# Checking four guessed recurrence streams on TensorE and ScalarE, and sharing the final adds out anew

## The chip, the cores and the metric

The kernel runs on one core of a Trainium2 chip. The metric is device time in microseconds (us). The engines are PE (TensorE, matrix products), PEld (its weight loads), DVE (VectorE), ACT (ScalarE), POOL (GpSimd) and SP (SyncE, which here only issues DMAs).

## The reference, cut to what matters

The input x is (16, 32, 32, 32) in fp32. First an attention-like block over a layer norm of x is added to x; then comes a feed-forward block that holds a recurrence over 1024 tokens:

```
x = x + conv_ref(ln(x), ...)            # scores, softmax, weighted values
t = x.reshape(16, 1024, 32)
Wx = batchnorm(ln(t) @ W.T) * gamma + beta
y = 0
for each token: y = sigmoid(Wx_t + y @ V.T); ys.append(y)
out = t + ys
```

The loop is sequential: each of its 1024 states needs the one before.

## The kernel before, in words

Everything stays in the on-chip memory of 128 partitions. Images and features lie on the partitions (G = 4 groups of C = 32), and the four groups of images Q = 4, the rows i and the columns lie along the free axis. The attention block, the second layer norm (`x2` is what the recurrence's result is added to) and the batch norm fill the time up to about 106 us.

**The recurrence.** It is not run token after token. The 1024 tokens are cut in 128 segments of SEG = 8, and all segments run at once, as STREAMS = 4 streams that each hold 32 segments of 4 groups of images (128 columns). A segment doesn't know the state it starts from, so ROUNDS = 17 rounds are run: WARM = 9 rounds, which run the tokens ahead of a segment from a guess and leave the start states in `warm`, and then 8 rounds whose states are kept in `states`. In each round and for each stream PE multiplies the last state by V (L1186) into a PSUM bank that was seeded with Wx (L933 on DVE), and ACT takes the sigmoid (L680). The four streams follow one another in the order that `order(WARM)` gives.

**The end.** A stream keeps 8 rows, and they are finished in PIECES: rows 0 to 3, rows 4 and 5, rows 6 and 7. For each piece `finish` (L945) waits for the states, transposes them 32x32 on DVE into `back` (`turn_back`, L356), and then adds `x2` (`add_back`, L362, one line for both engines). The list ON_DVE says which adds DVE does: one of the four of the first piece, and two of four of the others. POOL does the other seven. So DVE's program at the end is: 4 transposes of 128x512, one add of 512 columns, 4 transposes of 128x256, two adds of 256, 4 transposes of 256, two adds of 256, and then the check.

**The check.** The start states that were guessed are right if the last kept state of each segment agrees with the warm-up's last. DVE takes the difference of the 128x512 states (L965), squares and sums it along each partition (L969), and compares each partition's sum with AGREE squared, 2 to the power of -36 (L972). PE counts the partitions that agree (L1190), DVE turns the count into a flag (L974), and every engine but POOL loads the flag into a register (L345 on SP, L977 on DVE, L686 on ACT, L1192 on PE) and branches. When any partition disagrees, a loop of 127 passes over all streams computes the recurrence again; else the branch is skipped.

**The stores.** SP issues eight stores of 256 KB (L341): first rows 0 to 3 of each stream, then rows 4 to 7 of each, each after its adds (`wait_added`). It loads the flag only after it has issued all of them, and ends when they have landed. POOL's last work is its adds; before them it sets constants early on (`average`, L405) and works in the attention block and the layer norms.

Of the kernel before, what the change touches and what calls it, by code (L numbers as in the profile page):

```python
# [5 lines left out]
P = 128  # L6
G = 4
Q = 4
C = 32
# [16 lines left out]
ON_DVE = [(0, 3), (1, 1), (1, 3), (2, 1), (2, 3)]  # L26
PIECES = [(0, 4), (4, 2), (6, 2)]
STORES = [(0, 0, 4), (2, 4, 4)]
AGREE = 2.0 ** -18
LN1_EPS = 1e-6  # L30
LN2_EPS = 1e-5
# [10 lines left out]
def metaformer_kernel(nc, x, Wq, Wk, Wv, rq, rk, rv, Gq, Gk, Gv1, Gv2, W, V, gamma, beta, out):  # L42
# [4 lines left out]
    with ExitStack() as ctx:  # L47
        def sb(name, shape, dt=F32):
            return ctx.enter_context(nc.sbuf_tensor(name, shape, dt))
# [59 lines left out]
        nought = sb("nought", [P, C])  # L109
        ones = sb("ones", [P, 1])  # L110
        blank = sb("blank", [P, BANK], BF16)
        bn = sb("bn", [P, UNITS, 6])
        bnv = sb("bnv", [P, 8])
        std, scl, shift = (bnv[:, k:k + 1] for k in range(5, 8))
# [6 lines left out]
        diff = square[:, :, :].rearrange("p b (k m) -> p (b k) m", k=2)  # L121
# [6 lines left out]
        names = """x_in0 x_in1 x_in2 x_in3 x_in4 wqk_in w_in r_in_s rv_in gates_in gates2_in affine_in zeros average_set  # L128
# [10 lines left out]
        diff_d diff_sum agreed agree_count flag  # L139
        f_marked f_start f_seeded f_preact f_state f_turned""".split()  # L140
        S = {n: sem(n) for n in names}
        block = ctx.enter_context(nc.Block())
# [87 lines left out]

            return STREAMS * t + order(t).index(r) + 1

        STORED = 16 * len(STORES) * STREAMS
        FINAL_SIDE = side(WARM - 1)
        WARM_BANK = 0

# [28 lines left out]
            else:  # L265
                eng.wait_ge(S["seeded"], DVE_SEEDED.index((n, r)) + 1)

        def added_on_dve(n, r):

            return (n, order(WARM).index(r)) in ON_DVE  # L270

        ADDS = [(n, r) for n in range(len(PIECES)) for r in order(WARM)]

        def wait_added(eng, n, r):

            for own in (True, False):
                before = [k for k, a in enumerate([a for a in ADDS if added_on_dve(*a) == own]) if a[1] == r and a[0] <= n]
                if before:
                    eng.wait_ge(S["added_dve"] if own else S["added_pool"], before[-1] + 1)

        @block.sync
        def _(sp):
# [51 lines left out]
            for n in range(CHUNKS):  # L334
                spread_att(n)

            for n, row, k in STORES:
                for r in order(WARM):
                    wait_added(sp, n, r)
                    rows = slice(SEG * r + row, SEG * r + row + k)  # L340
# [9 lines left out]
            sp.wait_ge(S["stored"], STORED)  # L350

        def turn_back(row, k, r):

            rows = slice(SEG * r + row, SEG * r + row + k)
            at = P * (SEG * r + row)
            return nc.vector.transpose(back[:, at:at + P * k].rearrange("p (q i j) -> p i q j", q=Q, i=k),  # L356
                                       states[:, rows, :, :])

        def add_back(eng, row, k, r):
            rows = slice(SEG * r + row, SEG * r + row + k)  # L360
            at = P * (SEG * r + row)
            return eng.tensor_tensor(result[:, :, rows, :], back[:, at:at + P * k].rearrange("p (q i j) -> p q i j", q=Q, i=k),  # L362
                                     x2[:, :, rows, :], ALU.add)

        @block.gpsimd
        def _(pool):
# [37 lines left out]
            for k in range(1 - G, G):  # L404
                nc.gpsimd.affine_select(out=average[:, :, :], in_=average[:, :, :], compare_op=ALU.not_equal,  # L405
                                        fill=1.0 / G, base=C * k, pattern=[[-C, G], [-1, C]],
                                        channel_multiplier=1).then_inc(S["average_set"], 1)
                pool.wait_ge(S["average_set"], k + G)

            def shift_scores(n):  # L410
                pool.wait_ge(S["score_max"], n + 1)
# [52 lines left out]
            scale(6)  # L464
            scale(7)

            for n, r in ADDS:
                if not added_on_dve(n, r):
                    pool.wait_ge(S["turned_back"], ADDS.index((n, r)) + 1)
                    add_back(nc.gpsimd, *PIECES[n], r).then_inc(S["added_pool"], 1)  # L470

        @block.scalar
        def _(act):
# [198 lines left out]
            for t in range(ROUNDS):  # L672
                for r in order(t):
                    if t == 0:

                        nc.scalar.activation(state_out(t, r), wx_q[:, SEG * r + round_row(t), :, :],  # L676
                                             ACT.Sigmoid, bias=first_shift, scale=scl).then_inc(S["state"], 1)
                    else:
                        act.wait_ge(S["preact"], count(t, r) - STREAMS)
                        nc.scalar.activation(state_out(t, r), rec_slot(t, r).rearrange("p (q c) -> p q c", q=Q),  # L680
                                             ACT.Sigmoid).then_inc(S["state"], 1)
                if t == 0:
                    act_seeds(0)

            act.wait_ge(S["flag"], 1)
            repeat = act.value_load(repeat_flag[0:1, 0:1], min_val=0, max_val=1)  # L686
# [10 lines left out]
        def _(dve):  # L697
# [245 lines left out]
                    seed(n, r).then_inc(S["seeded"], 1)  # L943

            def finish(n):  # L945

                row, k = PIECES[n]
# [3 lines left out]
                for r in order(WARM):  # L951
                    if added_on_dve(n, r):
                        dve.wait_ge(S["turned_back"], ADDS.index((n, r)) + 1)
                        add_back(nc.vector, row, k, r).then_inc(S["added_dve"], 1)


            for n in range(len(SEEDS)):
                seeds(n)
            for n in range(len(PIECES)):
# [14 lines left out]
            nc.vector.tensor_scalar(repeat_flag[:, :], ps[0:1, 0, 0:1], float(P), None,  # L974
                                    ALU.is_lt).then_inc(S["flag"], 1)
            dve.wait_ge(S["flag"], 1)
            repeat = dve.value_load(repeat_flag[0:1, 0:1], min_val=0, max_val=1)  # L977
            with dve.If(repeat == 1):
                PASS = SEG * STREAMS
                dve.wait_ge(S["f_marked"], 1)  # L980
                with dve.Fori(0, SEGMENTS - 1) as n:

                    nc.vector.tensor_copy(warm[:, FINAL_SIDE, :, :, 1:C + 1], states[:, SEG - 1::SEG, :, :]).then_inc(S["f_start"], 1)
                    for h in range(GROUPS):
                        for r in range(STREAMS):
                            seed(len(SEEDS) - GROUPS + h, r).then_inc(S["f_seeded"], 1)
                    dve.wait_ge(S["f_state"], n * PASS + PASS)
                dve.wait_ge(S["stored"], STORED)
                for h in range(GROUPS):
                    for r in range(STREAMS):  # L990
                        n = GROUPS * (STREAMS * h + r)
                        turn_back(ROWS * h, ROWS, r).then_inc(S["f_turned"], 1)
                        dve.wait_ge(S["f_turned"], n + 1)
                        add_back(nc.vector, ROWS * h, ROWS, r).then_inc(S["f_turned"], 1)
                        dve.wait_ge(S["f_turned"], n + 2)

        @block.tensor
        def _(pe):
# [181 lines left out]
            for t in range(1, ROUNDS):  # L1180
                for r in order(t):
                    if t == 1 or SEED_OF[t] > SEED_OF[t - 1]:
# [52 lines left out]
```

## Time and profile before

| | us |
|---|---|
| runs of the kernel | 134.37, 137.07, 137.10 (median 137.07) |
| the profiled execution | 134.09 |
| its span, first to last instruction | 132.3 |
| granted TensorE clock, mean share of full | 0.98 |
| POOL, DVE, PE, ACT busy | 67.9, 95.3, 101.9, 79.4 |

The span is what the trace covers; the 1.8 us between it and the 134.09 us lie around it. A time "at 122.84" is counted from the start of the span. Where neighbouring instructions on DVE or POOL overlap by some hundredths, the later one's start is in the pipeline of the one before.

### The profile page before, as it was taken

What the parts mean: (1) busy time and instruction counts of PE and PEld (TensorE: products, weight loads), DVE (VectorE), ACT (ScalarE), POOL (GpSimd) and SP (SyncE); (2) the same over time, 40 slices, a digit from 0 to 9 for tenths busy, and PEclk for the clock granted to TensorE, in tenths of its full rate; (3) what the DMA queues carried; (4) which work ended last, traced back from release to release, by engine and by line L of the source; (5) the groups of instructions that cost most, each with busy time, mean ns of one, the idle gap of its engine ahead of it and who ended that gap; (6) DMA issues with size and microseconds to landing.
All of it is one profiled execution on the core that took longest, in us unless ns stands there. A gap on an engine that the chain in (4) does not pass through costs nothing.

```text
span 132.3 us, 4756 instructions
## 1 busy us (share of the span) xinstructions
PE 101.9 (77%) x2078; PEld 74.9 (57%) x2080; DVE 95.3 (72%) x151; ACT 79.4 (60%) x162; POOL 67.9 (51%) x77
## 2 busy tenths in 40 slices
PE   0694997799779999887995996756959969999000
PEld 0331232169779999775994995421312449999000
DVE  5898928857210396897790595799999597889991
ACT  7967874970913546598892512442652699999100
POOL 8996863994000057528700998998960000008840
PEclk9999999999999999999999999999999999999975
DMA  3892651084000000060061000000000000002666
GB/s 147 249 319 23 152 126 40 0 202 128 0 5 5 5 7 5 9 143 19 5 136 27 5 5 5 5 0 0 0 0 0 0 0 0 5 2 58 198 178 201
DMA packets 7968, 7.98 MB, mean 60 GB/s; under 512 B 2124, under 2 KB 6220, under 8 KB 7948
## 3 DMA queue, kind: packets, MB, share of 16 engines
q1 hardware_dynamic: 7948, 7.69, 22.0%
q8 instruction: 16, 0.26, 0.9%
q14 instruction: 4, 0.03, 0.1%
HBM read 2.97 MB, written 2.10 MB: 38 GB/s over the span
## 4 chain that ended last, share of the span: by engine, by line
PE 25%; POOL 22%; DVE 22%; ACT 13%; issue 7%; DMA 6%; SPq 2%; POOLq 0%; ACTq 0%; DVEq 0%
POOL y_tile L437 6%; ACT warm L680 5%; PE ps L1036 5%; PE ps L1072 4%; POOL u_tile L431 4%; DVE xin L356 4%; POOL y_tile L443 4%; PE ps L1051 4%; PE ps L1084 3%; DVE y_tile L362 3%; PE ps L1028 3%; POOL y_tile L196 3%; DMA spread_parts<-rel_tile 3%; PE ps L1060 3%; DMA xin<-in_x_dram 3%
## 5 line engine op out<-in xcount | busy, mean ns | idle before, releaser
L412 POOL TENSOR_TENSOR att_tile<-att_tile,soft 128x1024 f32<-128x1024 f32 x4 | 7.8, 1955 | 20.6 <-DVE soft L784 20.6
L362 POOL TENSOR_TENSOR y_tile<-xin,u_tile 128x256 f32<-128x256 f32 (+1 forms) x7 | 7.1, 1045 | 20.8 <-DVE xin L356 20.8
L1036 PE MATMUL ps<-spread_parts,u_tile 128*32 128x64 f32 x512 | 12.9, 252 | 2.0 <-issue 2.0
L1036 PEld LDWEIGHTS ps<-spread_parts,u_tile 128*32 128x32 f32 x512 | 12.2, 190 | 2.4 <-issue 2.4
L933 DVE TENSOR_SCALAR ps<-att_tile,bnv 128x512 f32<-128x512 f32 x15 | 11.0, 807 | 1.6 <-ACT warm L680 1.6
L1072 PE MATMUL ps<-spread_parts,rv_t 128*32 128x128 f32 x256 | 11.2, 339 | 0.9 <-DMA spread_parts<-rel_tile 0.9
L1084 PE MATMUL ps<-spread_parts,v_tile 128*32 128x64 f32 x512 | 9.0, 222 | 3.3 <-issue 3.2
L1095 PE MATMUL ps<-rel_tile,w_bd 128*128 128x512 f32 x16 | 8.7, 623 | 3.2 <-DVE rel_tile L848 2.5
L1072 PEld LDWEIGHTS ps<-spread_parts,rv_t 128*32 128x32 f32 x256 | 10.3, 119 | 1.4 <-issue 1.1
L1148 PE MATMUL ps<-blank 128*128 128x512 bf16 x40 | 9.8, 379 | 1.5 <-DVE u_tile L826 1.3
L778 DVE TENSOR_TENSOR att_tile<-ps,rel_tile 128x1024 f32<-128x1024 f32 x4 | 4.9, 1214 | 8.4 <-ACT rel_tile L513 8.4
L611 ACT ACTIVATE square<-y_tile 128x512 f32<-128x512 f32 x8 | 5.0, 628 | 9.6 <-POOL y_tile L437 9.6
L1084 PEld LDWEIGHTS ps<-spread_parts,v_tile 128*32 128x32 f32 x512 | 8.4, 109 | 3.9 <-issue 3.8
L1028 PE MATMUL ps<-y_tile,m_fac 32*32 32x512 f32 x64 | 7.7, 592 | 3.8 <-DVE y_tile L196 2.0
L1051 PE MATMUL ps<-spread_parts,r_fac 128*32 128x128 f32 x256 | 10.0, 315 | 0.0
L1008 PE MATMUL ps<-xin 128*128 128x512 f32 x18 | 9.9, 690 | 0.0
L1186 PE MATMUL ps<-warm,w_bd 128*128 128x128 f32 x72 | 9.0, 281 | 1.0 <-ACT warm L676 0.6
L513 ACT COPY rel_tile<-ps 128x512 f32<-128x512 f32 x8 | 4.8, 602 | 8.2 <-PE ps L1051 8.2
L1051 PEld LDWEIGHTS ps<-spread_parts,r_fac 128*32 128x32 f32 x256 | 9.6, 115 | 0.0
L583 ACT COPY spread_parts<-rel_tile 32x1024 f32<-32x1024 f32 x8 | 8.5, 1064 | 1.8 <-POOL rel_tile L419 1.5
L1186 PEld LDWEIGHTS ps<-warm,w_bd 128*128 128x128 f32 x72 | 8.4, 191 | 1.9 <-DVE ps L933 1.5
L431 POOL TENSOR_TENSOR u_tile<-att_tile,u_tile 128x512 f32<-128x512 f32 x4 | 5.2, 1330 | 7.4 <-ACT att_tile L604 7.4
(112 smaller groups left out, 242.2 us busy)
## 6 DMA issues: line engine op xcount, KB each, us to landing
out_dram<-y_tile SPq DMA_DIRECT2D x8, 256.0 KB, 2.3
xin<-in_x_dram SPq DMA_DIRECT2D x3, 512.0 KB, 4.6
spread_parts<-att_tile SPq DMA_DIRECT2D x8, 128.0 KB, 2.4
spread_parts<-rel_tile SPq DMA_DIRECT2D x8, 128.0 KB, 2.8
xin<-in_x_dram SPq DMA_DIRECT2D x2, 256.0 KB, 2.8
spread_parts<-u_tile SPq DMA_DIRECT2D x4, 128.0 KB, 2.3
att_tile<-in_L_conv_rv_dram SPq DMA_DIRECT2D x4, 128.0 KB, 3.0
att_tile<-in_L_conv_rq_dram SPq DMA_DIRECT2D x1, 128.0 KB, 6.1
```

The costliest lines, as they stand in the source:

```text
L362: return eng.tensor_tensor(result[:, :, rows, :], back[:, at:at + P * k].rearrange("p (q i j) -> p q i j", q=Q, i=k), x2[:, :, rows, :], A ...
L431: nc.gpsimd.tensor_tensor(unit(x2, k), first_sums[:, k, :, :], unit(x2, k), ALU.add).then_inc(S["x2_added"], 1)
L933: return nc.vector.tensor_scalar(out, rows, scl, shift, ALU.mult, ALU.add)
L1008: ins = nc.tensor.matmul(bank(k), xin[:, 0, 0:4, :].rearrange("p i j -> p (i j)"), xin[:, 0, 0:16, :].rearrange("p i j -> p (i j)"), start ...
L1028: ins = nc.tensor.matmul(bank(SIDE[k])[p, :], m_fac[p, :], y_tile[p, IMG * q + BANK * k:IMG * q + BANK * (k + 1)], start=True, stop=True)
L1036: return nc.tensor.matmul(ps[group(q), first + j // 8, at:at + G * HALF].rearrange("p (g i) -> p g i", g=G), u[:, q, :, j], y_bd[:, q, :, ...
L1051: ins = nc.tensor.matmul(side_bank(n)[group(q), P * k:P * (k + 1)].rearrange("p (g jp t) -> p g jp t", g=G, t=RUN), r_fac[:, ROWS * n + k, ...
L1072: ins = nc.tensor.matmul(bank(4 + n % 4)[group(g), P * k:P * (k + 1)].rearrange("p (q jp t) -> p q jp t", q=Q, t=RUN), rv_t[:, ROWS * n + ...
L1084: ins = nc.tensor.matmul(ps[group(g), first + j // 8, at:at + Q * HALF].rearrange("p (q i) -> p q i", q=Q), v_t[:, j, g, :], att_bd[:, g, ...
L1095: nc.tensor.matmul(bank(WX_BANK[k % 2]), w_bd[:, 1, :], by_row(tokens, k), start=True, stop=True).then_inc(S["wx_product"], 1)
L1148: ins = nc.tensor.matmul(bank(k), blank[:, 0:P], blank[:, :], start=True, stop=True)
L1186: nc.tensor.matmul(rec_slot(t, r), w_bd[:, 2, :], state_in(t, r), start=False, stop=True, skip_group_check=True).then_inc(S["preact"], 1)
```

## The change

The check leaves DVE. POOL makes a 128x128 unit matrix and its negative early on (`signs`). When all states are there, PE multiplies the last states by the first and the warm-up's last states by the second, both into PSUM bank 1, which then holds the difference; ACT squares that bank with a sum along each partition. DVE keeps the two small comparisons, and they now stand between its adds. PIECES, ON_DVE and STORES go: the transposes keep the three pieces (TURNED), with rows 4 to 7 written into one block of `back`; POOL adds rows 0 to 3 of all four streams, and DVE adds rows 4 to 7 of all four, in one instruction of 512 columns each, after all its transposes. The stores are the same eight.

```diff
+TURNED = [(0, 4), (4, 2), (6, 2)]
...
         def wait_added(eng, n, r):
+            eng.wait_ge(S["added_dve" if n else "added_pool"], order(WARM).index(r) + 1)
...  (SP)
-            for n, row, k in STORES:
+            for n in range(GROUPS):
                 for r in order(WARM):
                     wait_added(sp, n, r)
...
         def turn_back(row, k, r):
+            at = COLS // C * (SEG * r + row - row % ROWS)
+            block4 = back[:, at:at + BANK].rearrange("p (q i j) -> p i q j", q=Q, i=ROWS)
+            return nc.vector.transpose(block4[:, row % ROWS:row % ROWS + k], states[:, SEG * r + row:SEG * r + row + k, :, :])
...  (POOL, early)
+            nc.gpsimd.memset(signs[:, :, :], 0.0).then_inc(S["signs_zero"], 1)
+            pool.wait_ge(S["signs_zero"], 1)
+            for n, unit_value in enumerate((1.0, -1.0)):
+                nc.gpsimd.affine_select(out=signs[:, n, :], in_=signs[:, n, :], compare_op=ALU.not_equal, fill=unit_value, base=0,
+                                        pattern=[[-1, P]], channel_multiplier=1).then_inc(S["signs_set"], 1)
...  (POOL, end)
+            for i, r in enumerate(order(WARM)):
+                pool.wait_ge(S["turned_back"], i + 1)
+                add_back(nc.gpsimd, 0, r).then_inc(S["added_pool"], 1)
...  (ACT, after the recurrence)
+            act.wait_ge(S["diff_product"], 1)
+            nc.scalar.activation(square[:, 0, 0:BANK], bank(1), ACT.Square, accum_out=diffsum[:, :]).then_inc(S["diff_sum"], 1)
...  (DVE)
-            dve.wait_ge(S["state"], STREAMS * ROUNDS)
-            nc.vector.tensor_tensor(diff[:, 0, :].rearrange("p (r q c) -> p r q c", r=STREAMS, q=Q),
-                                    states[:, SEG - 1::SEG, :, :], warm[:, FINAL_SIDE, :, :, 1:C + 1],
-                                    ALU.subtract).then_inc(S["diff_d"], 1)
-            dve.wait_ge(S["diff_d"], 1)
-            nc.vector.tensor_tensor_reduce(diff[:, 1, :], diff[:, 0, :], diff[:, 0, :], 1.0, 0.0,
-                                           ALU.mult, ALU.add, diffsum[:, :]).then_inc(S["diff_sum"], 1)
+            def finish_adds(streams):
+                for i, r in streams:
+                    dve.wait_ge(S["turned_back"], STREAMS * (len(TURNED) - 1) + i + 1)
+                    add_back(nc.vector, 1, r).then_inc(S["added_dve"], 1)
...
+            streams = list(enumerate(order(WARM)))
+            finish_adds(streams[0:2])
             dve.wait_ge(S["diff_sum"], 1)
             nc.vector.tensor_scalar(agreed[:, :], diffsum[:, :], AGREE * AGREE, None, ALU.is_le).then_inc(S["agreed"], 1)
+            finish_adds(streams[2:3])
             dve.wait_ge(S["agree_count"], 1)
             nc.vector.tensor_scalar(repeat_flag[:, :], ps[0:1, 0, 0:1], float(P), None,
                                     ALU.is_lt).then_inc(S["flag"], 1)
+            finish_adds(streams[3:4])
...  (PE)
+            pe.wait_ge(S["signs_set"], 2)
+            pe.wait_ge(S["state"], STREAMS * ROUNDS)
+            nc.tensor.matmul(bank(1).rearrange("p (r m) -> p r m", r=STREAMS), signs[:, 0, :],
+                             states[:, SEG - 1::SEG, :, :].rearrange("p r q c -> p r (q c)"), start=True, stop=False)
+            nc.tensor.matmul(bank(1).rearrange("p (r q c) -> p r q c", r=STREAMS, q=Q), signs[:, 1, :],
+                             warm[:, FINAL_SIDE, :, :, 1:C + 1], start=False, stop=True).then_inc(S["diff_product"], 1)
```

## Rows read from the trace of the kernel before

**Rows 1.** The page's chain that ended last, shares of the span by engine.
```profile
PE 25%; POOL 22%; DVE 22%; ACT 13%; issue 7%; DMA 6%; SPq 2%; POOLq 0%; ACTq 0%; DVEq 0%
```

**Rows 2.** Timeline of ACT from 115.7 us: start us, us, engine, line, operation, count.
```profile
115.61 7.23 ACT L680 ACTIVATE v_tile<-ps 128x128 f32<-128x128 f32 x32
```

**Rows 3.** The chain of waits after 115 us: start us, us it adds, what.
```profile
118.60 2.50 DVE xin L356 x4
121.12 1.31 DVE y_tile L362
122.44 1.33 DVE xin L356 x4
123.77 1.62 DVE y_tile L362 x2
125.39 1.33 DVE xin L356 x4
126.72 1.12 DVE y_tile L362 x2
127.84 0.61 DVE square L965
128.48 0.69 DVE square L969
129.65 0.14 DVE repeat_flag L974
```

**Rows 4.** Lines 977 and 47, sequencer instructions: count, ns min/median/max, first and last start.
```profile
L977 DVEq TENSOR_LOAD <-repeat_flag x1: 1177/1177/1177, 129.8 to 129.8; - x1
L47 SPq DRAIN  x1: 13/13/13, 131.8 to 131.8; - x1
L47 DVEq DRAIN  x1: 51/51/51, 132.0 to 132.0; - x1
```

**Rows 5.** Line 341, the sixth and the last store, each with its time to landing.
```profile
L341 SPq DMA_DIRECT2D out_dram<-y_tile x1: 373/373/373, 127.5 to 127.5; - x1
DMA to landing us min/median/max: 2.3/2.3/2.3
...
L341 SPq DMA_DIRECT2D out_dram<-y_tile x1: 543/543/543, 128.5 to 128.5; - x1
DMA to landing us min/median/max: 3.1/3.1/3.1
```

**Rows 6.** Busy time by window: PE, PEld, DVE, ACT, POOL, PEclk, DMA share, GB/s.
```profile
123.00:127.00 4.00, 0.00 (x0) 0.00 (x0) 4.00 (x10) 0.00 (x0) 3.28 (x5) 1.00 0.64 188
127.00:132.00 5.00, 0.19 (x2) 0.09 (x2) 2.44 (x7) 0.00 (x0) 0.23 (x1) 0.51 0.73 210
```

**Rows 7.** Timeline of the adds between 119 and 123 us, read in narrow windows.
```profile
119.39 1.27 POOL L362 TENSOR_TENSOR y_tile<-xin,u_tile 128x512 f32<-128x512 f32 x1 [20.05 <-DVE xin L356]
120.62 1.26 POOL L362 TENSOR_TENSOR y_tile<-xin,u_tile 128x512 f32<-128x512 f32 x1
121.12 1.31 DVE L362 TENSOR_TENSOR y_tile<-xin,u_tile 128x512 f32<-128x512 f32 x1
121.85 1.71 POOL L362 TENSOR_TENSOR y_tile<-xin,u_tile 128x512 f32<-128x512 f32 x1
```

**Rows 8.** Timeline: one fp32 product of 512 columns (L1095) on PE, and ACT's nearest operations.
```profile
96.36 1.10 PE L1095 MATMUL ps<-rel_tile,w_bd 128*128 128x512 f32 x2 [0.59 <-ACT att_tile L624]
...
91.17 0.63 ACT L611 ACTIVATE square<-y_tile 128x512 f32<-128x512 f32 x1 [0.78 <-POOL y_tile L437]
...
104.80 1.28 ACT L658 ACT_TABLE_LOAD   x1
106.09 0.20 ACT L658 ACTIVATE table_load<-bn_eps 128x1 f32<-128x1 f32 x1
```

**Rows 9.** Timeline of POOL from 27 us: the constants, and the idle time behind them.
```profile
28.97 3.05 POOL L405 TENSOR_SCALAR_AFFINE_SELECT average<-average 128x128 f32<-128x128 f32 x7
47.78 1.95 POOL L412 TENSOR_TENSOR att_tile<-att_tile,soft 128x1024 f32<-128x1024 f32 x1 [15.77 <-DVE soft L784]
```

More of the change, by code:

```diff
@@ L25 @@
 LN_PARTS = [(0, 0, 16), (0, 16, 16), (1, 0, 32), (2, 0, 32), (3, 0, 32)]
-ON_DVE = [(0, 3), (1, 1), (1, 3), (2, 1), (2, 3)]
-PIECES = [(0, 4), (4, 2), (6, 2)]
-STORES = [(0, 0, 4), (2, 4, 4)]
+TURNED = [(0, 4), (4, 2), (6, 2)]
 AGREE = 2.0 ** -18
@@ L111, in metaformer_kernel @@
         blank = sb("blank", [P, BANK], BF16)
+        signs = sb("signs", [P, 2, P])
         bn = sb("bn", [P, UNITS, 6])
@@ L120, in metaformer_kernel @@
         table_load = sb("table_load", [P, 1])
-        diff = square[:, :, :].rearrange("p b (k m) -> p (b k) m", k=2)
         agreed = sb("agreed", [P, 1])
@@ L126, in metaformer_kernel @@
         ps = ctx.enter_context(nc.psum_tensor("ps", [P, 8, BANK], F32))
-        names = """x_in0 x_in1 x_in2 x_in3 x_in4 wqk_in w_in r_in_s rv_in gates_in gates2_in affine_in zeros average_set
+        names = """x_in0 x_in1 x_in2 x_in3 x_in4 wqk_in w_in r_in_s rv_in gates_in gates2_in affine_in zeros average_set signs_zero signs_set
         spread_zero0 spread_zero1 spread_zero2 spread_zero3 y_in0 y_in1 y_in2 y_copied_dve y_copied_act att_in0 att_in1 att_copied
@@ L138, in metaformer_kernel @@
         warm_zero warmed seeded preact state turned_back added_dve added_pool stored
-        diff_d diff_sum agreed agree_count flag
+        diff_product diff_sum agreed agree_count flag
         f_marked f_start f_seeded f_preact f_state f_turned""".split()
@@ L231, in count @@
             return STREAMS * t + order(t).index(r) + 1
-        STORED = 16 * len(STORES) * STREAMS
+        STORED = 16 * GROUPS * STREAMS
         FINAL_SIDE = side(WARM - 1)
@@ L266, in wait_seeded @@
                 eng.wait_ge(S["seeded"], DVE_SEEDED.index((n, r)) + 1)
-        def added_on_dve(n, r):
-            return (n, order(WARM).index(r)) in ON_DVE
-        ADDS = [(n, r) for n in range(len(PIECES)) for r in order(WARM)]
         def wait_added(eng, n, r):
[L276 to L279, printed above, removed]
+            eng.wait_ge(S["added_dve" if n else "added_pool"], order(WARM).index(r) + 1)
         @block.sync
@@ L335, in _ @@
                 spread_att(n)
-            for n, row, k in STORES:
+            for n in range(GROUPS):
                 for r in order(WARM):
                     wait_added(sp, n, r)
-                    rows = slice(SEG * r + row, SEG * r + row + k)
+                    rows = slice(SEG * r + ROWS * n, SEG * r + ROWS * (n + 1))
                     sp.dma_start(out_dram[:, :, C * rows.start:C * rows.stop],
@@ L352, in turn_back, with add_back @@
         def turn_back(row, k, r):
[L354 to L362, printed above, removed]
+            at = COLS // C * (SEG * r + row - row % ROWS)
+            block4 = back[:, at:at + BANK].rearrange("p (q i j) -> p i q j", q=Q, i=ROWS)
+            return nc.vector.transpose(block4[:, row % ROWS:row % ROWS + k], states[:, SEG * r + row:SEG * r + row + k, :, :])
+        def add_back(eng, n, r):
+            rows = slice(SEG * r + ROWS * n, SEG * r + ROWS * (n + 1))
+            at = COLS // C * rows.start
+            return eng.tensor_tensor(result[:, :, rows, :], back[:, at:at + BANK].rearrange("p (q i j) -> p q i j", q=Q, i=ROWS),
                                      x2[:, :, rows, :], ALU.add)
@@ L465, in _ @@
             scale(7)
[L467 to L470, printed above, removed]
+            for i, r in enumerate(order(WARM)):
+                pool.wait_ge(S["turned_back"], i + 1)
+                add_back(nc.gpsimd, 0, r).then_inc(S["added_pool"], 1)
         @block.scalar
@@ L945, in finish @@
             def finish(n):
-                row, k = PIECES[n]
+                row, k = TURNED[n]
                 for r in order(WARM):
@@ L950, in finish @@
                     turn_back(row, k, r).then_inc(S["turned_back"], 1)
[L951 to L954, printed above, removed]
+            def finish_adds(streams):
+                for i, r in streams:
+                    dve.wait_ge(S["turned_back"], STREAMS * (len(TURNED) - 1) + i + 1)
+                    add_back(nc.vector, 1, r).then_inc(S["added_dve"], 1)
             for n in range(len(SEEDS)):
                 seeds(n)
-            for n in range(len(PIECES)):
+            for n in range(len(TURNED)):
                 finish(n)
-            dve.wait_ge(S["state"], STREAMS * ROUNDS)
-            nc.vector.tensor_tensor(diff[:, 0, :].rearrange("p (r q c) -> p r q c", r=STREAMS, q=Q),
-                                    states[:, SEG - 1::SEG, :, :], warm[:, FINAL_SIDE, :, :, 1:C + 1],
-                                    ALU.subtract).then_inc(S["diff_d"], 1)
-            dve.wait_ge(S["diff_d"], 1)
-            nc.vector.tensor_tensor_reduce(diff[:, 1, :], diff[:, 0, :], diff[:, 0, :], 1.0, 0.0,
-                                           ALU.mult, ALU.add, diffsum[:, :]).then_inc(S["diff_sum"], 1)
+            streams = list(enumerate(order(WARM)))
+            finish_adds(streams[0:2])
             dve.wait_ge(S["diff_sum"], 1)
             nc.vector.tensor_scalar(agreed[:, :], diffsum[:, :], AGREE * AGREE, None, ALU.is_le).then_inc(S["agreed"], 1)
+            finish_adds(streams[2:3])
             dve.wait_ge(S["agree_count"], 1)
@@ L993, in _ @@
                         dve.wait_ge(S["f_turned"], n + 1)
-                        add_back(nc.vector, ROWS * h, ROWS, r).then_inc(S["f_turned"], 1)
+                        add_back(nc.vector, h, r).then_inc(S["f_turned"], 1)
                         dve.wait_ge(S["f_turned"], n + 2)
```

## The prediction

> **What bounds the kernel now.** I read the page's chain first: no engine holds more than a quarter of it [rows 1], so a change at one place is worth what the last wait at that place is worth, and nothing more. The change leaves everything before the last states alone, apart from three constants on POOL. So I read ACT's timeline for the moment from which the tail runs: 32 sigmoids in 7.23 us, one each 0.22 us, the last of them ending at 122.84 [rows 2]. That moment stays. From there the chain of waits is DVE alone: transposes and adds until 127.84, the difference and its square for about 1.3 us, then the two small comparisons, with the flag at 129.79 [rows 3]. That would say: take work off DVE and gain all of it.
>
> Two more views say that it isn't so. The sequencer rows show that loading the flag takes 1.18 us and that DVE drains at 132.0, just before the end at 132.25; SP drains at 131.85 [rows 4]. So two paths end together: flag to end is 132.25 - 129.83 = 2.42 us on DVE, and the stores are the other. The last store is issued at 128.54 and lands 3.1 us later, at 131.64; the sixth, issued at 127.54, needs only 2.3 and lands at 129.84 [rows 5]. The eighth is two places behind the sixth: (131.64 - 129.84) / 2 = 0.90 us a store. That is a queue: a store issued while another is under way lands 0.90 us after it, not 2.3 us after its issue. The window after 127 us has the DMA engines busy for 73% of the time, a stretch of it without any store [rows 6]. So a faster flag is worth nothing unless the stores come earlier too, and how early they come is set by when each add ends.
>
> **The change, part by part.**
>
> *Constants on POOL.* A memset and two selects over 128x128; seven such selects took 3.05 us, 0.44 each [rows 9], so some 1.3 us. POOL idles for 15.77 us behind them [rows 9]. They cost nothing; without that cover they would cost their 1.3 us.
>
> *DVE's transposes.* The first four end at 121.10, as now [rows 3]. The add that follows goes, so the eight small ones come next: two groups of four at 1.33 us [rows 3] end at 121.10 + 2.66 = 123.76. The last round's states are there at 122.16 to 122.84 (0.22 apart, back from the last, rows 2), and the last group starts at 122.43, so it never waits for one. Their writes into blocks of four rows change only a step; I cost that at nothing.
>
> *POOL's adds.* Four of 512 columns, at 1.23 us from start to start [rows 7], from 119.39: the fourth ends at 119.39 + 4 x 1.23 + 0.04 = 124.35. Now the first store group is complete at 124.0, since DVE does one of the four; this is the part that becomes slower.
>
> *DVE's first two adds.* A DVE add beside a POOL add is not free: at 121.12 it took 1.31 us, ending at 122.43, where the POOL add before it ended at 121.88; the difference is 0.55, the time of an add by itself (0.61 for L965, rows 3). And the POOL add that began at 121.85 took 1.71 in place of 1.27 [rows 7]. I read this as turns, not as sharing: whoever starts second stands still. So the first DVE add, issued at 123.7, waits for POOL and ends at 124.35 + 0.55 = 124.90; the second, undisturbed, at 125.51. If both were slowed instead, POOL's fourth would end 0.44 later, at 124.8. The Trainium skill ("SBUF — State Buffer", section "Who interferes with whom") says that a VectorE instruction with two SBUF inputs and a GpSimd instruction that reads SBUF exclude one another for the whole instruction, first come first served; by it POOL's fourth add isn't lengthened, and the trace agrees, with 1.26 us for the POOL add that the DVE add ran into.
>
> *The check on PE and ACT.* No product of this kind is in the trace. One fp32 product of 512 columns took 1.10 us [rows 8], two 2.20; the lower bound is that the second is hidden in the pipeline by half, about 1.6, the upper that PE has fallen to 1.2 GHz, 4.4. PE stands idle for 4 us after the recurrence at a granted clock of 1.00 and only in the next window is it 0.51 [rows 6], and here it gets work at once: I take 2.20, and PE ends at 122.84 + 0.05 + 2.20 = 125.09. ACT's square of 512 columns took 0.63 [rows 8]; reading out the sum is not shown, between 0.08 (DVE's whole step behind L969 takes no more) and a small ACT instruction of 0.20 [rows 8]; I take 0.20, the like engine. The sum is there at 125.96. What waits behind it on DVE is two adds and, through them, the last two stores.
>
> *DVE's end.* It stands 0.4 us for the sum, compares (0.15) until 126.15, adds until 126.76, sets the flag (0.14, rows 3) at 126.90, with PE's count long done in between, and adds until 127.51. The flag load follows at 127.54 at the latest and ends the program on DVE at 127.54 + 2.42 = 129.96.
>
> *The stores.* With 2.3 us for one that meets none and 0.90 behind another: the fourth is issued at 124.38 and lands at 126.7. The fifth (124.93) would land at 127.2 and is queued to 127.6, the sixth (125.54) to 128.5, the seventh (126.79) to 129.4, the eighth (127.54) to 130.3, where by itself it would have landed at 129.85. SP issues the same eight instructions, each some 0.4 us, so none is delayed by the queue's own time. A delay of the check up to 0.45 us is thus hidden.
>
> *The sum.* The last landing was 131.64 with the end at 132.25; SP's drain comes 0.2 after the landing, and the final barrier takes 0.2 to 0.25. The new end is 130.3 + 0.45 = 130.75, and DVE's path, 129.96, is covered by 0.8. That is 1.5 us less than the 132.25, or 132.6 for the profiled execution of 134.09. The runs lie at 134.4 once and at 137.1 twice, so the median stands 3.0 above the profiled execution for reasons that no row shows; the forecast for a median is **137.07 - 1.5 = 135.6 us**, 1.1% less.
>
> **The rivals.**
>
> *A. The gain is smaller, because the fourth POOL add or the check comes late.* Slowed by DVE, POOL's fourth ends at 124.8; every later store moves by 0.44 and the end is 131.2, a gain of 1.05. For it: 1.71 us in [rows 7]. Or a function table is loaded for the square: the table is the sigmoid's, and one load took 1.28 us [rows 8]. If it stands behind ACT's wait, the sum comes at 127.24, the last add ends at 128.79, and the last store lands at 128.8 + 2.3 = 131.1, or 131.2 in the queue: a gain of 0.6. Against it: the squares of the norms ran without a load of their own beside the square root. Time: 136.0 to 136.5.
>
> *B. The gain is larger.* If the queue's 0.90 shrinks when stores come more evenly spaced, the last lands at 129.85 and the end is 130.3, or DVE's own 129.96 if SP's end is quicker: a gain of 2.0 to 2.3, 134.8 to 135.1. Against it: stores five to seven still come within 2.3 us of each other.
>
> *C. Tables change twice around the square,* to its set and back to the sigmoid's, both between ACT's wait and the sum: 2 x 1.28 = 2.57 us [rows 8]. The sum comes at 128.53, the eighth store is issued at 130.11 and lands at 132.4, and the end is 132.85: **slower by 0.6 us**, 137.7. It decides when the sum comes 2.0 us or more after my 125.96, since 132.25 - 0.45 - 2.3 = 129.5 is the latest issue that costs nothing, 1.96 after mine. For the price of a change of table the trace has 1.28 us, the activation behind it starting 0.01 later [rows 8]. The Trainium skill ("ScalarE: Activation LUTs", section "What ACT_TABLE_LOAD costs") adds a drain and calls a change about 2.66 us; by this one change alone would make the kernel slower by some 0.7 us. The trace doesn't show that drain.
>
> *D. The products don't reproduce the difference exactly,* so that a partition exceeds 2 to the power of -36 and the repeat loop runs. The limit over 512 elements is a root mean square of 2^-18 / 22.6 = 1.7e-7, near the last bits of an fp32 number below 1, so rounding in the products could reach it. The price: 127 passes of 8 rounds of 4 sigmoids at 0.22 us [rows 2] are at least 894 us, over 1,030 in all. Against it: a product with one and minus one has nothing to round if PE carries all bits, and the two PE instructions for each fp32 product [rows 8] speak for that.
>
> **How the numbers follow.** The forecast has 0.58, A 0.20, B 0.12, C 0.06, D 0.04. The likeliest, 135.6, stands. For the range: the runs before lie at two levels, 134.1 to 134.4 and 137.1, and the new kernel may fall on either. On the lower B gives 134.2 - 2.2 = 132.0; on the upper A's small end gives 136.5 and no gain 137.1. I take 132.0 to 137.2; C and D are left out. A measurement of this kernel can tell about 2% from no change, 2.7 us here. No case gives that much gain by its own; the two levels of the runs could, if the medians fall apart: faster 0.17. Slower by over 2% are D and the wrong fall of the levels: 0.07. Within 2%: 0.76.
>
> **What would show it.** In the profile after: the last sigmoid at about 122.8; eight transposes back to back until 123.8; four POOL adds, none over 1.3 us, until 124.35; the first DVE add ending near 124.9; PE's products until 125.1 and no ACT_TABLE_LOAD before the square; a wait on DVE of some 0.4 us before line L972's successor; the flag at 126.9 against 129.8; the last store issued at 127.5 and landing 2.8 us later; the end by SP and not by DVE. The prediction is wrong if the recurrence itself ends at another time, if the queue lands stores other than 0.9 apart, or if DVE stands for over 0.9 us at the sum.

## The result, and the profile after

The changed kernel runs in 133.69 us (median of 20 runs) against 135.16 for the kernel before on 20 runs. The fast runs of both, compared alone, give a ratio of 0.988, with a 95% interval of 0.984 to 0.992. It is faster by about 1.5 us; the interval allows 1.1 to 2.1. Forecast were 1.5 us and a ratio of 0.989. The level forecast, 135.6 us, rested on the first three runs of the kernel before and was 1.9 us too high; each kernel's runs scatter over some 4 us. The changed kernel's profiled execution took 134.51 us, with a span of 132.7.

The spans can't be compared as they stand: in the changed kernel's trace the last sigmoid ends 1.6 us later than in the one before, at 124.44 in place of 122.84 [rows 2], though nothing on its path was changed. In the 14 traces of this study that moment lies anywhere from 121.7 to 125.0. So I count everything from there. The time from the last sigmoid's end to the end of the span, the **tail**, is 9.42 us before and 8.25 after, 1.17 less.

The chain of waits at the end of the changed kernel (start us, us it adds, what):

```profile
124.00 0.46 ACT v_tile L673 x2
...
124.59 1.10 PE ps L1181 x2
125.69 0.87 PE ps L1183 x2
126.58 0.70 ACT square L679 x2
127.30 0.15 DVE agreed L959
127.45 0.60 DVE y_tile L350
128.11 0.60 DVE y_tile L350
```

DVE's difference and square of [rows 3] are gone, and two adds stand behind the sum that PE and ACT now make. The timeline of the same stretch, each engine's part of it:

```profile
121.00 4.96 POOL L350 TENSOR_TENSOR y_tile<-xin,u_tile 128x512 f32<-128x512 f32 x4 [20.06 <-DVE xin L345]
...
125.23 1.28 DVE L350 TENSOR_TENSOR y_tile<-xin,u_tile 128x512 f32<-128x512 f32 x1
...
127.07 0.19 ACT L679 ACTIVATION_READ_ACCUMULATOR square<-ps 128x1 f32 x1
127.30 0.15 DVE L959 TENSOR_SCALAR agreed<-diffsum 128x1 f32<-128x1 f32 x1 [0.19 <-ACT square L679]
127.97 0.14 DVE L962 TENSOR_SCALAR repeat_flag<-ps 1x1 int32<-1x1 f32 x1
```

POOL's four adds keep their 1.24 us each; where [rows 7] had one of 1.71, none is lengthened. DVE's first add starts while POOL's fourth is under way and takes 1.28. No ACT_TABLE_LOAD stands before the square, and DVE waits 0.19 us for the sum. The last two stores (line 331) with their times to landing, and the sequencers' ends:

```profile
L331 SPq DMA_DIRECT2D out_dram<-y_tile x1: 372/372/372, 128.1 to 128.1; - x1
DMA to landing us min/median/max: 3.0/3.0/3.0
...
L331 SPq DMA_DIRECT2D out_dram<-y_tile x1: 462/462/462, 128.7 to 128.7; - x1
DMA to landing us min/median/max: 3.6/3.6/3.6
...
L966 DVEq TENSOR_LOAD <-repeat_flag x1: 1154/1154/1154, 128.1 to 128.1; - x1
L45 DVEq DRAIN  x1: 45/45/45, 130.3 to 130.3; - x1
L45 SPq DRAIN  x1: 13/13/13, 132.5 to 132.5; - x1
```

The drains stand at the end of each engine's program. In [rows 4] DVE drained last, at 132.0, with SP at 131.85. Now DVE is done 2.2 us ahead of SP: the flag's path is far off the end, and the stores alone set it. The last one takes 3.6 us to land, although it is issued 0.65 us behind the seventh.

The steps in numbers, in us after the end of the last sigmoid (a store has landed when its semaphore is raised):

| | forecast | changed | before |
|---|---|---|---|
| transposes done | 0.92 | 0.87 | 3.9 |
| POOL's last add of rows 0 to 3 | 1.51 | 1.52 | 0.7 |
| DVE's first, second add of rows 4 to 7 | 2.06, 2.67 | 2.07, 2.67 | |
| PE's products, sum ready | 2.25, 3.12 | 2.10, 2.82 | |
| flag | 4.06 | 3.66 | 6.96 |
| last store issued | 4.70 | 4.29 | 5.70 |
| stores 4 to 8 landed | 3.86, 4.76, 5.66, 6.56, 7.46 | 3.91, 4.80, 5.73, 6.63, 7.86 | 3.96, 6.09, 7.05, 7.97, 8.85 |
| end of the span | 7.91 | 8.25 | 9.42 |

### The profile page after: what moved, and what is told of

It reads as the page before. It is cut to its first block, busy times and chain, and to the rows that moved or that the text cites. A ratio compares the mean times of both kernels' runs of the same rounds, so it can differ in the third digit from the quotient of the medians.

```text
span 132.7 us, 4763 instructions
## 1 busy us (share of the span) xinstructions
PE 104.9 (79%) x2082; PEld 76.5 (58%) x2084; DVE 92.8 (70%) x147; ACT 79.7 (60%) x164; POOL 66.6 (50%) x77
## 4 chain that ended last, share of the span: by engine, by line
PE 30%; POOL 22%; ACT 17%; DVE 11%; issue 7%; DMA 5%; SPq 4%; POOLq 0%; ACTq 0%
PE ps L1040 7%; POOL y_tile L431 6%; ACT v_tile L673 5%; ACT warm L673 5%; PE ps L1025 5%; PE ps L1061 4%; POOL u_tile L425 4%; POOL y_tile L437 4%; PE ps L1073 3%; DMA xin<-in_x_dram 3%; PE ps L1017 3%; POOL y_tile L195 3%; PE ps L1049 3%; SPq L297 2%; DMA spread_parts<-rel_tile 2%
## 5 line engine op out<-in xcount | busy, mean ns | idle before, releaser
L350 POOL TENSOR_TENSOR y_tile<-xin,u_tile 128x512 f32<-128x512 f32 x4 | 5.0, 1271 | 20.1 <-DVE xin L345 20.1
L997 PE MATMUL ps<-xin 128*128 128x512 f32 x18 | 10.7, 745 | 0.0
```

The source lines that it names most:

```text
L997: ins = nc.tensor.matmul(bank(k), xin[:, 0, 0:4, :].rearrange("p i j -> p (i j)"), xin[:, 0, 0:16, :].rearrange("p i j -> p (i j)"), start ...
```

## The experiments

All tails below are read in one profile per kernel. They are steadier than the times: two profiles of the changed kernel gave 8.25 and 8.28, two of the candidate (run 7) 7.32 both times, but two of the kernel with the later flag (run 5) 7.91 and 8.12, while the times of one kernel scatter by 4 us. A difference of 0.2 us between two tails is thus not safe where the last store is what differs. Where a timed ratio disagrees with a tail, I say so.

**1. The check alone.** The adds, the transposes and the stores of before, the check of after:

```diff
-            dve.wait_ge(S["state"], STREAMS * ROUNDS)
-            nc.vector.tensor_tensor(diff[:, 0, :]...).then_inc(S["diff_d"], 1)
-            dve.wait_ge(S["diff_d"], 1)
-            nc.vector.tensor_tensor_reduce(diff[:, 1, :], ...).then_inc(S["diff_sum"], 1)
+   (PE's two products, ACT's square, POOL's signs as in the change)
```

> Only the check moves to PE and ACT; the adds and stores stay as before. I count from the end of the last sigmoid to the end of the span: 9.42 us before, 8.25 us in the changed kernel. Theory Q (the end is set by the store queue: a store lands 2.3 us after its issue, or 0.9 us after the store before it): the stores are issued as before, the last lands 8.85 us after the last sigmoid, and the tail is 9.2 us, a gain of 0.2 us. Theory D (DVE's time until the flag sets the end, the flag plus 2.42 us): DVE loses 1.4 us and the tail is 8.0 us.

The tail was 9.64 us, the ratio 1.005 (0.999 to 1.012). Theory D, 8.0 us, is out: taking 1.4 us off DVE gained nothing. Theory Q's stores came as expected, except for the last, which landed at 9.24 in place of 8.85, so the tail grew by 0.2 us in place of shrinking by as much:

```profile
L341 SPq DMA_DIRECT2D out_dram<-y_tile x1: 547/547/547, 128.2 to 128.2; - x1
DMA to landing us min/median/max: 3.5/3.5/3.5
```

**2. The adds alone.** From the changed kernel; DVE's check goes behind its four adds:

```diff
-            finish_adds(streams[0:2])
+            finish_adds(streams)
+            (line 964 to 970 of the kernel before: the difference and its square on DVE)
             dve.wait_ge(S["diff_sum"], 1)
-            finish_adds(streams[2:3])
-            finish_adds(streams[3:4])
```

> Only the adds and stores move; the check stays on DVE, behind all adds. Theory Q: the adds end 2.1, 2.7, 3.3 and 3.9 us after the last sigmoid, the last store lands at 7.5 as in the forecast, and the flag, at 5.95, ends the kernel at 8.4 by its own 2.42 us: a tail of 8.4 us, 1.0 less than before, so most of the change's gain is the adds'. Theory D says the same 8.4 here only if the flag is late; it would give the adds no part in the changed kernel's gain of 1.2 us beyond DVE's shorter list of instructions.

The tail was 8.10 us, the ratio 0.988 (0.973 to 1.003). The last store landed at 7.48. The adds by themselves give 1.32 us, more than the whole change. The flag at 5.82 ended it, as expected; its path took 2.28 us and not 2.42.

**3. The changed kernel again.** No edit.

> The changed kernel once more. In its first profile the last store landed 1.23 us after the seventh, where the others stood 0.90 apart. If that was chance, it lands 0.9 us after it here and the tail is 7.9 us; if it belongs to this order of stores, the tail is 8.2 us again.

The last store landed 1.25 us behind the seventh and the tail was 8.28 us: no chance. The ratio was 0.995 (0.989 to 1.001), whose interval meets the first comparison's.

**4. No check.** The two products and the square are left out:

```diff
+            nc.gpsimd.memset(diffsum[:, :], 0.0).then_inc(S["diff_sum"], 1)     (POOL, early)
-            (PE's two products, ACT's square)
```

> The two products and the square are left out and the sum is set to zero early, so DVE never waits for it; the two comparisons, the count and the flag stay. Theory Q: the last two adds end 0.2 to 0.4 us earlier, the store queue hides it, and the tail stays that of the changed kernel, 7.9 to 8.2 us. The rival (DVE's wait for the sum is paid in full): 0.2 to 0.4 us less.

Both were wrong. The tail grew to 9.65 us, with less work in it, and the timed ratio agrees: 1.000 (0.994 to 1.006), no gain left over the kernel before. The last store was issued 4.01 us after the last sigmoid, earlier than in the changed kernel, and took 5.2 us; it landed 2.6 us behind the seventh. What else moved? The flag, to 3.39, the earliest of all. The page names two DMA queues of kind "instruction". Here is what each holds from 129.0 us on (packets, MB, share of 16 engines), after the store's bulk has passed at 129.1:

```profile
q1 hardware_dynamic: 128, 0.06, 8.1%
q8 instruction: 1, 0.02, 2.2%
q14 instruction: 1, 0.01, 0.7%
```

and the windows of that end (PE, PEld, DVE, ACT, POOL, PEclk, DMA share, GB/s):

```profile
128.00:129.00 1.00, 0.00 (x0) 0.00 (x0) 0.00 (x0) 0.00 (x0) 0.00 (x0) 0.50 1.02 286
129.00:130.00 1.00, 0.00 (x0) 0.00 (x0) 0.00 (x0) 0.00 (x0) 0.00 (x0) 0.50 0.27 78
130.00:130.90 0.90, 0.00 (x0) 0.00 (x0) 0.00 (x0) 0.00 (x0) 0.00 (x0) 0.50 0.04 5
```

The queue runs full until 129, then nearly empties, and a last few packets of 512 bytes pass after 130. Between lies the 16 KB instruction packet, from 129.40 to 130.37 in its record. From 130.38 us on eight packets start, all of them the last store's:

```profile
DMA packets 8, 0.00 MB, mean 6 GB/s; under 512 B 1, under 2 KB 8, under 8 KB 8
```

Theory F came from here: the branch behind the flag makes an engine fetch instructions, and a part of the last store stands behind the fetch on one of the DMA engines. In this run the packets bear that out. In the changed kernel they don't as it stands: its last data packet ends at 7.40 and its 16 KB packet starts at 7.41, and from 131.86 us on no packet starts:

```profile
DMA packets 0, 0.00 MB, mean 0 GB/s; under 512 B 0, under 2 KB 0, under 8 KB 0
```

So no packet of that store waited behind the large one, and yet it landed 0.35 us later than in run 6 below, which has no fetch. Its last five data packets end 0.047 us apart, the last of them at 7.40 in place of 7.16, and the landing follows 0.46 us behind it in place of 0.35. Why is open.

**5. The flag later.** All adds ahead of the comparisons:

```diff
-            finish_adds(streams[0:2])
+            finish_adds(streams)
             (agreed)
-            finish_adds(streams[2:3])
             (flag)
-            finish_adds(streams[3:4])
```

> The changed kernel with all four of DVE's adds ahead of the two comparisons, so the flag comes at 4.5 us after the last sigmoid in place of 3.66. Theory F: after the branch the engines fetch instructions by DMA (16 KB, 0.96 us of one DMA engine); where that is asked for while the last store is still under way, some 2.5 us after the flag and before 7.1, a part of the last store stands behind it and it lands 1.23 us after the seventh and not 0.9. Here the fetch is asked for at about 7.0: the last store lands at 7.5 and the tail is 7.9 us, 0.35 less than the changed kernel, though the flag is later. Rival (the flag's time costs or is hidden, no fetch): the tail stays 8.25 us or grows.

The flag came at 4.37 in place of 3.66, the last store landed at 7.52, 0.88 us behind the seventh, and the tail was 7.91 us: 0.34 less for a later flag. The last store of this kernel:

```profile
L331 SPq DMA_DIRECT2D out_dram<-y_tile x1: 853/853/853, 127.5 to 127.5; - x1
DMA to landing us min/median/max: 3.6/3.6/3.6
```

It was issued 0.4 us earlier than the changed kernel's and would have landed no earlier for that in the queue; what it gained is the 0.34. A repetition (12 below) kept only 0.13 of it.

**6. No branch.** The flag is computed, but nobody loads it, and the repeat loops are left out:

```diff
-            X.wait_ge(S["flag"], 1)
-            repeat = X.value_load(repeat_flag[0:1, 0:1], min_val=0, max_val=1)
-            with X.If(repeat == 1): ...      (X: SP, ACT, DVE, PE)
```

> The changed kernel without the four loads of the flag and without the repeat loops behind them (the flag is still computed). Theory F: no jump, no late fetch, the last store lands 0.9 us after the seventh at 7.5 and the tail is 7.9 us or a little under. Rival (the last store is slow in this order of stores whatever follows): it lands at 7.86 and the tail is 8.2 us.

With all issues where the changed kernel has them (the last at 4.29), the last store landed at 7.51 and the tail was 7.92 us. The answer on DMAs for its tail, from 124.0 us to the end, names one queue alone:

```profile
DMA packets 4120, 2.04 MB, mean 230 GB/s; under 512 B 128, under 2 KB 4120, under 8 KB 4120
## 3 DMA queue, kind: packets, MB, share of 16 engines
q1 hardware_dynamic: 4120, 2.04, 79.8%
```

No instruction packet, no delay. The edit takes out the loads of the flag, the branches and the code of the loops together, so it doesn't say by itself which of them it is. The loads alone are unlikely: in run 2 DVE's lies at 5.86 to 6.86, while the data of the last two stores move, and the last was not late. The timed ratio, 0.999 (0.995 to 1.004), doesn't show the 1.5 us that the tail lost. The trace has its last sigmoid at 124.97, the latest of all; whether the shorter program makes the part before slower is open.

**7. POOL adds three.** A candidate, 11 a repetition of it:

```diff
+TURNS = 4 of (0, i), 4 of (1, i), then (2, 0) to (2, 3)
+DVE_ADDS = [(0, 2), (1, 0), (1, 1), (1, 2), (1, 3)]
+POOL_ADDS = [(0, 0), (0, 1), (0, 3)]
...  (DVE)
+            turn(0, 0) ... turn(0, 3); turn(1, 0); turn(1, 1)
+            add(0, 2)
+            turn(1, 2); turn(1, 3); turn(2, 0); turn(2, 1)
+            add(1, 0); add(1, 1)
+            turn(2, 2); turn(2, 3)
+            add(1, 2); add(1, 3)
+            (agreed, flag)
```

> A candidate. DVE adds rows 0 to 3 of the third stream between its transposes, POOL the other three; the transposes of the last two rows alternate with DVE's adds; the check comes after all adds. Theory Q with F: the third and fourth stores are issued at -0.4 and 0.75 us against 0.32 and 1.55 now, the fifth at 1.5, the last at 3.95; the queue lands the last at 6.65, the flag is there at 4.55 and ends DVE at 6.85: a tail of 7.0 to 7.1 us, 1.2 us less than the changed kernel and 2.3 less than before (1.7%). Rival (POOL and DVE slow each other, so that moving an add to DVE delays its transposes and every store): a tail of 8.2 us or more.

The tail was 7.32 us and the ratio 0.987 (0.979 to 0.995). The issues came as expected (-0.35, 0.77, 1.55, ... 4.01), the landings didn't: from the second store on, at 1.46, they stand 0.87 to 0.95 apart to the last, at 6.93. I had let the queue begin with the fourth store. It begins with the second now, and the tail is the time to move 1.5 MB.

**8. Half of each store** (groups of images 0 and 1 alone):

```diff
-                    sp.dma_start(out_dram[:, :, C * rows.start:C * rows.stop], result[:, :, rows, :]...)
+                    sp.dma_start(out_dram[:, 0:2, C * rows.start:C * rows.stop], result[:, 0:2, rows, :]...)
```

> The changed kernel with half of each store left out (two of the four groups of images, 128 KB each). Theory Q: a store occupies the DMA engines for 0.45 us and not 0.9, no store stands behind another, and the last lands 2.0 to 2.3 us after its issue at 4.29, at 6.3 to 6.6. Rival (the spacing of 0.9 us is the cost of one store instruction whatever its size): the last lands at 7.5 to 7.9 again.

```profile
L331 SPq DMA_DIRECT2D out_dram<-y_tile x1: 372/372/372, 127.9 to 127.9; - x1
DMA to landing us min/median/max: 1.8/1.8/1.8
```

The last landed 1.81 us after its issue, at 6.10, and the tail was 6.49 us: it landed 0.2 us sooner than expected, since a store that meets none is itself 0.5 us shorter. The 0.9 us is the time that 256 KB take, about 290 GB/s, not the cost of an instruction.

**9. The check late:**

```diff
+            for _ in range(3):
+                nc.tensor.matmul(bank(1)..., signs[:, 0, :], states..., start=True, stop=False)
+                nc.tensor.matmul(bank(1)..., signs[:, 1, :], warm..., start=False, stop=True)
```

> The changed kernel with PE's pair of products made four times over before ACT squares the bank, 0.86 us a pair, so the sum comes 2.6 us later, at about 5.4 us after the last sigmoid in place of 2.83. Theory Q: the seventh and the last store are issued at 6.2 and 6.9 us, the last lands 2.3 us after its issue, at 9.2, and the tail is 9.6 us, 1.3 more than the changed kernel (1.7 more than with a last store at 7.5): half or more of a late check is paid, since two adds stand behind it. Rival (the check is hidden behind the store queue however late): 8.25 us.

I had mis-sized the edit: 0.86 us is one product back to back, not a pair (the chain above adds 0.87 for the second), so the sum came 5.15 us later, at 7.97. By Q's own rule with the stores issued at 8.78 and 9.44, the last lands at 12.0 and the tail is 12.4. The tail was 14.28: the last store took 4.45 us:

```profile
L331 SPq DMA_DIRECT2D out_dram<-y_tile x1: 372/372/372, 131.2 to 131.2; - x1
DMA to landing us min/median/max: 4.4/4.4/4.4
```

The instruction packet ran from 11.90 to 12.86, and three packets of the last store end behind it, at 12.92 to 13.04. That is theory F's delay once more, 1.9 us of it, in a queue that had stood empty before. The windows around it (same columns):

```profile
132.50:133.60 1.10, 0.00 (x0) 0.00 (x0) 0.00 (x0) 0.00 (x0) 0.00 (x0) 0.50 0.72 206
133.60:134.60 1.00, 0.00 (x0) 0.00 (x0) 0.00 (x0) 0.00 (x0) 0.00 (x0) 0.50 0.06 17
```

**10. The candidate with the check on DVE:**

```diff
             add(1, 2); add(1, 3)
+            (the difference and its square on DVE)
             (agreed, flag)
```

> The candidate with POOL adding three, but with the check back on DVE, behind all adds. Theory Q with the flag's path: the stores stay (the last lands at 6.9), the flag comes 1.95 us after the last add, at 5.9, and the tail is 5.9 + 2.3 = 8.2 us, 0.9 more than the candidate: with the stores early, the check's place is worth what it is not worth with the stores late. Rival (the stores alone set the end): 7.3 us.

The tail was 7.76 us, 0.44 more than the candidate and not 0.9. The flag came at 5.94 as expected, but its path took 1.8 us and not 2.3 (below).

**11 and 12. The candidate and the later flag, timed again.**

> The candidate once more, timed longer and on the same chip as the next kernel. Its tail was 7.32 us against 7.91 of the one with the later flag: 0.6 us or 0.4% less than that, 2.1 us or 1.6% less than the kernel before.

> The changed kernel with all adds ahead of the comparisons, once more. Tail 7.9 us, 1.5 us or 1.1% less than the kernel before; the fetch starts at 7.1 us or later and the last store lands 0.9 us after the seventh.

The candidate again had 7.32 us and a ratio of 0.987 (0.977 to 0.997), the lowest of all beside run 7's, though the changed kernel's 0.988 lies well within its interval. The later flag had 8.12 us this time: the last store landed 1.09 us behind the seventh. Its 16 KB packet starts at 7.26, at the edge of the last store's packets, and the delay is partly back, so 4.4 us is not late enough to be safe. Its ratio was 0.995 (0.990 to 1.000), against 0.988 (0.977 to 0.999) in the first comparison. One of its runs took 325.89 us at a clock of 1.00; nothing here explains it, and the repeat loop would take over 1,030.

## Why the prediction was right

The number is better than the working behind it. The medians are 1.5 us apart, as forecast, but the tail shrank by 1.17 us and not by 1.50, and the changed kernel timed again (run 3) gave a ratio of 0.995, some 0.7 us. The 1.17 lies within the first interval, so the two don't contradict each other; that the medians fell on 1.5 is in part luck. Two of the text's own signs of being wrong came true, a recurrence that ends at another time and stores that land other than 0.9 apart. The mechanism holds but for the last store.

- **Two ends, both moved.** The flag's path and the stores ended together before. Run 1 moved the flag by 1.45 us and not the stores, and gained nothing; run 2 moved the stores, and the flag by 1.14 us, and gained 1.32 us. That the gain lies in how early the stores are issued is shown; their order is the same. The gain is less than the flag's 3.3 us, as forecast.
- **The queue.** Landings were forecast as the later of issue + 2.3 and the one before + 0.90. For stores four to seven of the changed kernel this is within 0.07 us. In run 8 stores of half the size landed 0.56 and 0.59 us apart, as they were issued, so the 0.90 goes with the bytes and isn't a price of each instruction.
- **POOL and DVE take turns.** The forecast put POOL's fourth add at 1.51 and DVE's first at 2.06; it was 1.52 and 2.07. The DVE add ends 0.55 us behind POOL's, as before. POOL's add was not lengthened although a DVE add waited on it, as the rule of the Trainium skill ("SBUF — State Buffer", section "Who interferes with whom") has it, that the later one stands still for the whole instruction; the sharing of rival A would have given 1.96 for POOL. In the candidate (run 11) a DVE add came between two of POOL's, and POOL's next took 1.71 us, as in [rows 7]:

```profile
121.10 0.78 DVE L357 TENSOR_TENSOR y_tile<-xin,u_tile 128x512 f32<-128x512 f32 x1
121.30 1.71 POOL L357 TENSOR_TENSOR y_tile<-xin,u_tile 128x512 f32<-128x512 f32 x1
```

- **The check on PE and ACT.** Forecast 3.12, measured 2.82: the two products took 1.95 us from start to end and not 2.20, since the second begins before the first has ended, 0.93 us after its start. The square took 0.60 and not 0.63, and the readout's 0.20 was right (0.19), but it began 0.11 us before the square's end. Against that PE began 0.15 us behind the last sigmoid and not 0.05. It made the last issue 0.4 us earlier and, by the queue, nothing else.
- **The step that failed: "the eighth (127.54) to 130.3".** The last store was 0.90 behind the seventh by the forecast and 1.23 in the trace, 0.33 us of the 0.34 between a tail of 7.91 and one of 8.25. The text held that the flag's path was covered by 0.8 us and so harmless. It is not harmless: with the loads and the branches left out (run 6) the 0.33 us are gone, and with the flag earlier still (run 4) they become 1.7. An instruction fetch that follows the branch and comes close to the last store's data goes with every delay seen; how it delays the store in the changed kernel, where no packet stands behind it, is open. That the flag, 0.4 us sooner than forecast, made it worse is likely by runs 4, 5 and 12, but not shown.
- **The rivals.** A's load of a table, C and D didn't occur: the last table load is at 106.4 us, ahead of the recurrence, and the repeat didn't run. The drain that the Trainium skill ("ScalarE: Activation LUTs", section "What ACT_TABLE_LOAD costs") adds to a change of table was thus not put to the test. B, a queue much tighter than 0.90, was not seen in any run with whole stores; 0.86 was the least.
- **The runs' level.** "The recurrence itself ends at another time" did happen, by 1.6 us between the two traces. The first sigmoid starts anywhere from 105.1 to 108.3 us in the 14 traces, and the last ends 16.63 or 16.64 us later in every one, so this scatter arises before the recurrence. What in that part makes it is not settled. It is over twice as large as the gain. The level of 137.07 was the median of three runs, two of them high, and 20 runs put it at 135.16.

## What to carry to other kernels

Before work is taken off a busy engine at the end of a kernel, list every path that ends there and when each would end by itself; here the busy engine's path and the store queue ended within 0.2 us of each other, and only the queue was worth moving. Stores form a queue that is sized in bytes: issue the first as early as the data allow, since while they queue, later work on the engines is free as long as no store comes too late for its turn. And what is off the path can still collide with it: a branch brought a fetch of instructions by DMA, and the runs without a delay had it 0.5 us or more behind the last store's data (before, runs 2, 7, 10 and 11) or, once, right at their end (run 5). No run had it well ahead of them; the earliest flag (run 4) lost 1.7 us.

## What the runs showed of the hardware that I had not expected

- **A fetch of instructions behind a branch meets the stores.** How far the last store landed behind the seventh, by when the flag came, when the 16 KB packet began and when the last data packet of the stores ended (us after the last sigmoid):

| run | flag | 16 KB packet starts | last data packet ends | last store behind the seventh |
|---|---|---|---|---|
| 4 | 3.39 | 7.26 | 8.68 | 2.62 |
| 9 | 8.81 | 11.90 | 13.04 | 2.75 |
| changed, 3 | 3.66 | 7.41, 7.45 | 7.40, 7.44 | 1.23, 1.25 |
| 1 | 5.51 | 8.69 | 8.68 | 1.24 |
| 12 | 4.36 | 7.26 | 7.25 | 1.09 |
| 5 | 4.37 | 7.18 | 7.17 | 0.88 |
| 7, 11 | 4.48, 4.47 | 7.06, 7.12 | 6.58, 6.57 | 0.87, 0.88 |
| 2 | 5.82 | 8.33 | 7.13 | 0.88 |
| 10 | 5.94 | 7.94 | 6.58 | 0.88 |
| before | 6.96 | 9.63 | 8.50 | 0.87 |
| 6 | no branch | none | 7.16 | 0.87 |

  Without a fetch, or with one that begins 0.5 us or more after the store's data, the distance is 0.87 or 0.88. In runs 4 and 9 packets of the store end behind the 16 KB packet, and 1.7 and 1.9 us are lost. In the changed kernel and runs 1, 3, 5 and 12 the 16 KB packet starts within 0.01 us of the end of the last data packet, as if it had stood in line behind it, and 0 to 0.4 us are lost. The first of the four branches is ACT's; the packet starts 1.2 to 1.5 us behind its end where the store's data had passed (before, 2, 7, 10, 11), 1.4 and 1.6 us in runs 5 and 12, and 2.0 to 2.7 us in the changed kernel and runs 1, 3, 4 and 9. So the fetch is late where the store is late, which fits a line at one DMA engine that both stand in. On which of the 16 engines, what decides who goes first, and what delays the store where no packet of it stands behind the fetch, stays open.
- **Loading the flag has no fixed price.** DVE's load took 1.15 to 1.18 us in the changed kernel and the one before, 1.00 in run 2, 0.87 in the candidate, and 0.54 in runs 9 and 10. In run 9 no store's data were moving during it. In run 10, the candidate with DVE's check, they were: its load, and the window over it (DMA share 0.89, columns as above):

```profile
L982 DVEq TENSOR_LOAD <-repeat_flag x1: 543/543/543, 128.5 to 128.5; - x1
...
128.49:129.04 0.55, 0.00 (x0) 0.00 (x0) 0.00 (x0) 0.00 (x0) 0.00 (x0) 0.50 0.89 253
```

  So stores under way don't settle the price by themselves, and what does is open. A flag path of 2.42 us with a load of 1.18 in it was too long for run 10, whose load was 0.63 us shorter and whose path was 1.82; that is why it ended 0.4 us earlier than expected.
